# A windowed-attention and ternary-FFN block: output bias added by TensorE, remote bias and gate moved in their queues

## The chip, the core and the metric

The kernel runs on one NeuronCore of one Trainium2 chip. TensorE multiplies matrices and writes to PSUM; VectorE, ScalarE and GpSimd work on SBUF and (but for GpSimd) PSUM; SyncE issues the DMAs. Each engine runs its own instruction list in order, and they wait for each other by semaphores. The metric is the device time of one execution in microseconds.

## The reference

`x` is 16 sequences of 512 tokens of 256 numbers. One transformer block with the norms behind each half:

```
# local attention, 16 heads of 16, window of 128 (the token itself left out), per 128-token block
qkv = x @ qkv_w + qkv_b
local = softmax(where(allowed, q k^T / 4, -1e9)) v            # zero where nothing is allowed
# remote ("latent") attention: 64 pooled chunks of 8 tokens, 4 heads of 16
pooled = mean of x over chunks of 8;  rq = x @ rq_w + rq_b;  rk, rv = split(pooled @ rkv_w + rkv_b)
lat_out = softmax(where(chunk earlier, rq rk^T / 4, -1e9)) rv
remote = lat_out @ rout_w + rout_b                            # split into 16 heads of 16
gate = sigmoid(local @ gl_w + remote @ gr_w)                  # one number per token and head
mixed = gate * local + (1 - gate) * remote
x = layernorm(x + mixed @ out_w + out_b)
# FFN with ternary weights
h = gelu(ternary_linear(x, w_up));  x = layernorm(x + ternary_linear(h, w_down))
```

`ternary_linear` divides its input by its root mean square and multiplies by sign(w) where |w| is over half the mean of |w|, else 0.

## The kernel before

Everything of one sequence fits the chip; the kernel is a software pipeline over the 16 sequences, with the order of each engine's work written out by hand. Steps are named by a phase, a sequence and a number:

- **P** (projections of a sequence, two sequences ahead): `QK`..`QK+3` multiply x by the query and key weights (fp32, four 128x512 products each) into a PSUM bank. The scores need more than bf16 precision, so ScalarE turns each bank into bf16 parts: part 0 at `QK+c`; then TensorE subtracts it from the bank (`SPLIT` steps, a product with `minusb`), ScalarE makes part 1, TensorE subtracts, ScalarE makes part 2. `SPLIT+2t` and `SPLIT+2t+1` belong to tile t. SyncE stores the parts to DRAM and loads them back in stacks (`restack`). Then the latent attention: `LAT_RQ`, `LAT_RKV` (ScalarE: `rqT`, `lat_bd`; VectorE: `rv_bd`), `LAT_SCORES`, `LAT_EXP`, `LAT_NORM`, `LAT_T`, `LAT_O`, and `REMOTE`, `REMOTE+1`, which give `rem` (the remote result) and `remg` (its share of the gate). `VALUES`..`VALUES+3` compute v.
- **A** (22 steps): row maxima of the next sequence's scores, on TensorE and VectorE. `T` is `split_maxima`: they become two bf16 rows, which SyncE puts into the stacks with 16 small DMAs (`move_max`).
- **S, PV** (16 steps): transposed scores, exp on ScalarE, causal masks on GpSimd (`mask`, L656 and L660), weighing of v.
- **F** (second half of a sequence): `GATE` on VectorE (L1146 to L1189) with a tanh on ScalarE (L850), which leaves the mixture transposed in `mixT`; `OUT`, `OUT+1` (TensorE L1558: `mixT` times `wout`; VectorE L1197: adds `xres`, then statistics; GpSimd L670: the powers); `NORM`; `XN_T`, `XN_HI`, `XN_LO`: the normalised input is transposed and split into two f16 parts; GpSimd computes `x1`, the residual's scaling (L676), at `XN_HI`; `UP`..`UP+7` with down products two steps behind (L1544), GpSimd making `h_lo` (L684); `END`.

`SECOND_HALF` (L76) interleaves F of a sequence with P of the sequence two ahead, and all engines follow it. `order_of_prologue` (L133) orders what comes ahead of sequence 0: P of sequences 0 and 1, A of sequence 0, and preparations `W`: `FOLD`, `PREP` (VectorE's `prepare`, L945), `EDGES`, `SUMS`, `TERNARY`. Before sequence 0, ScalarE copies a gate bias at `EDGES`.

The output bias is folded on VectorE at `PREP`: `bout` (in all 128 rows) is out_b plus v's bias times out_w, and GpSimd adds it to the loaded residual `xres`, behind its last mask. Behind that it adds the remote bias of the next sequence:

```
                for b in range(NB):
                    add_bias(s, b)                     # L723, xres += bout, 128x256 each
                if s.next().exists and not s.first:
                    bias_remote(s.next())              # L713, rem += rem_b, two of 128x512
```

Sequence 0 has no such `bias_remote`: that of sequence 1 is in the prologue, at `REMOTE+1`.

## Time and profile before

| | |
|---|---|
| median of 3 runs | 1200.73 us (1200.21 to 1201.3) |
| profiled execution, own time | 1197.75 us |
| its span, first to last instruction | 1196.0 us |
| TensorE, weight loads | 994.4 us (83%), 626.9 us (52%) |
| VectorE, ScalarE, GpSimd | 854.5 us (71%), 744.4 us (62%), 672.6 us (56%) |
| mean granted TensorE clock | 0.960 of full |

In the rows, times are microseconds from the span's start; a row gives start, duration, engine, line, operation, output and input tile, their sizes, and how many alike are merged; in brackets stands how long the engine was idle ahead of it and what ended that. PE is TensorE, DVE VectorE, ACT ScalarE, POOL GpSimd, SPq SyncE's DMA issues. A row that merges several (x4) may span pauses between them.

### The profile page before, as it was taken

What the parts mean: (1) busy time and instruction counts of PE and PEld (TensorE: products, weight loads), DVE (VectorE), ACT (ScalarE), POOL (GpSimd) and SP (SyncE); (2) the same over time, 40 slices, a digit from 0 to 9 for tenths busy, and PEclk for the clock granted to TensorE, in tenths of its full rate; (3) what the DMA queues carried; (4) which work ended last, traced back from release to release, by engine and by line L of the source; (5) the groups of instructions that cost most, each with busy time, mean ns of one, the idle gap of its engine ahead of it and who ended that gap; (6) DMA issues with size and microseconds to landing.
All of it is one profiled execution on the core that took longest, in us unless ns stands there. A gap on an engine that the chain in (4) does not pass through costs nothing. (4 is left out here: it accounts for less than half of the span.)

```text
span 1196.0 us, 36957 instructions
## 1 busy us (share of the span) xinstructions
PE 994.4 (83%) x15353; PEld 626.9 (52%) x15368; DVE 854.5 (71%) x1772; ACT 744.4 (62%) x1189; POOL 672.6 (56%) x852
## 2 busy tenths in 40 slices
PE   6768898988888898888989888888988888894855
PEld 2445564655556464555646455564645555562433
DVE  4377686786868687696868778686877868686454
ACT  3524766767676665767676575757667675763544
POOL 6007375565747465474746646583664648374664
PEclk9888999999999999999999999999999999997877
DMA  6731513315061431506152341515234150601000
GB/s 187 199 98 56 152 46 115 101 46 150 23 177 39 132 83 62 152 15 166 39 153 62 92 123 38 142 39 153 61 98 118 38 143 21 176 22 38 1 18 19
DMA packets 58868, 107.45 MB, mean 90 GB/s; under 512 B 20518, under 2 KB 38726, under 8 KB 55622
## 3 DMA queue, kind: packets, MB, share of 16 engines
q1 hardware_dynamic: 58556, 105.08, 31.1%
q8 instruction: 121, 1.98, 0.7%
q14 instruction: 47, 0.39, 0.1%
q10 hardware_dynamic: 144, 0.00, 0.0%
HBM read 70.87 MB, written 33.55 MB: 87 GB/s over the span
## 5 line engine op out<-in xcount | busy, mean ns | idle before, releaser
L842 ACT ACTIVATE Pt<-scores 128x1024 f32<-128x1024 f32 (+1 forms) x256 | 229.9, 918 | 125.3 <-PE oacc L1531 79.6
L684 POOL TENSOR_TENSOR h_lo<-hbuf,h_hi 128x512 f16<-128x512 f32 x128 | 148.2, 1158 | 202.3 <-DVE h_hi L1231 202.3
L1104 DVE TENSOR_REDUCE nmax<-work 128x3 f32<-128x480 f32 x352 | 214.3, 632 | 28.8 <-PE work L1482 25.8
L656 POOL TENSOR_SCALAR_AFFINE_SELECT Pt<-Pt 128x512 f32<-128x512 f32 x256 | 165.3, 646 | 52.0 <-ACT Pt L842 51.6
L1531 PE MATMUL oacc<-Pt,Vp 128*32 128x256 f32 (+1 forms) x2048 | 152.9, 361 | 15.2 <-POOL Pt L660 9.8
L1361 PE MATMUL scores<-xT,wqk 128*128 128x512 f32 x256 | 125.5, 625 | 37.8 <-ACT parts L762 31.2
L1477 PE MATMUL work<-Ks,Qs 98*32 98x160 bf16 x4096 | 143.6, 235 | 13.2 <-DVE nmax L1104 10.1
L1508 PE MATMUL scores<-Qs,Ks 100*32 100x160 bf16 (+4 forms) x4096 | 118.3, 229 | 32.1 <-ACT Pt L842 17.6
L670 POOL TENSOR_TENSOR rs<-rs,power 128x6 f32<-128x6 f32 x32 | 42.6, 1333 | 176.1 <-DVE rs L1208 176.1
L1231 DVE CAST h_hi<-hbuf 128x512 f16<-128x512 f32 x128 | 68.2, 532 | 101.2 <-ACT hbuf L878 100.7
L1544 PE MATMUL oacc<-wdn_t,h_hi 128*128 128x256 f16 x512 | 118.1, 273 | 9.5 <-POOL h_lo L684 9.5
L660 POOL TENSOR_SCALAR_AFFINE_SELECT Pt<-Pt 128x512 f32<-128x512 f32 x192 | 122.7, 639 | 0.0
L1508 PEld LDWEIGHTS scores<-Qs,Ks 100*32 100x32 bf16 x4096 | 81.2, 97 | 78.6 <-ACT Pt L842 52.1
L1544 PE MATMUL oacc<-wdn_t,h_lo 128*128 128x256 f16 x512 | 117.9, 273 | 0.0
L878 ACT ACTIVATE hbuf<-work 128x512 f32<-128x512 f32 x128 | 76.0, 594 | 60.4 <-PE work L1596 58.9
L1477 PEld LDWEIGHTS work<-Ks,Qs 98*32 98x32 bf16 x4096 | 88.2, 96 | 38.4 <-DVE nmax L1104 27.9
L1596 PE MATMUL work<-xnT,wup_t 128*128 128x512 f16 x384 | 99.4, 381 | 5.7 <-DVE h_sum L1237 5.4
L769 ACT ACTIVATE parts<-scores,bqk 128x512 bf16<-128x512 f32 x128 | 87.7, 685 | 21.3 <-PE scores L1371 15.4
L1482 PE MATMUL work<-mask_band,identb 128*32 128x192 bf16 (+1 forms) x1408 | 99.5, 246 | 0.6 <-issue 0.5
L1237 DVE TENSOR_TENSOR h_sum<-h_sum,work 128x512 f32<-128x512 f32 x112 | 76.3, 682 | 10.8 <-ACT work L885 10.1
L676 POOL TENSOR_SCALAR x<-ytok,mv,rs 128x256 f32<-128x256 f32 x64 | 77.6, 1227 | 1.7
L1343 PE MATMUL scores<-wv,xT 128*128 128x272 f32 x256 | 73.4, 414 | 5.1 <-DVE wrog L972 5.1
(170 smaller groups left out, 1871.6 us busy)
## 6 DMA issues: line engine op xcount, KB each, us to landing
parts_scratch<-parts SPq DMA_DIRECT2D x96, 256.0 KB, 5.2
Qs<-parts_scratch SPq DMA_DIRECT2D x96, 256.0 KB, 4.9
Ks<-parts_scratch SPq DMA_DIRECT2D x96, 256.0 KB, 4.8
xT<-x_t SPq DMA_DIRECT2D x16, 512.0 KB, 3.9
xres<-x SPq DMA_DIRECT2D x16, 512.0 KB, 4.7
y<-nat SPq DMA_DIRECT2D x16, 512.0 KB, 3.0
Qs<-nmax_pair SPq DMA_DIRECT2D x256, 2.0 KB, 1.8
nat<-up_t SPq DMA_DIRECT2D x1, 1024.0 KB, 6.0
```

What stands on the lines that cost most here:

```text
L656: ins = pool.affine_select(out=pt[:, :, 0:P], in_=pt[:, :, 0:P], compare_op=ALU.is_gt, fill=0.0, base=0, pattern=[[0, 4], [1, P]], channel ...
L660: ins = pool.affine_select(out=pt[:, :, P:2 * P], in_=pt[:, :, P:2 * P], compare_op=ALU.is_ge, fill=0.0, base=0, pattern=[[0, 4], [-1, P]] ...
L684: pool.tensor_tensor(h_lo[:, t % NR, :], hbuf[:, t % 2, :], h_hi[:, t % NR, :], ALU.subtract).then_inc(h_lo_ready, 1)
L842: nc.scalar.activation(Pt[:, u % NPT, :, 0:w], scores[:, slot, :, :].rearrange("p k (h q) -> p (k h) q", h=2)[:, :, 0:w], ACT.Exp, scale=S ...
L1104: nc.vector.tensor_reduce(nmax[:, first:first + n], work[:, slot, 0:n * BAND].rearrange("p (h c) -> p h c", h=n), X, ALU.max, negate=True) ...
L1361: mm = nc.tensor.matmul(p_bank(bank), wqk[:, t, c * P:(c + 1) * P], xT[:, t, :], start=(t == 0), stop=False, skip_group_check=True)
L1477: nc.tensor.matmul(work[g * GT:(g + 1) * GT, slot, i * BAND:(i + 1) * BAND], q[0:KA, h, at:at + GT], kk[0:KA, h * S + at:h * S + at + BAND ...
L1482: mm = nc.tensor.matmul(o[:, :, 0:NG + 1:NG, :], identb[:, g * GT:(g + 1) * GT], mask_band[:, :, :].unsqueeze(1).to_broadcast([P, n, 2, GT ...
L1508: mm = nc.tensor.matmul(scores[g * GT:(g + 1) * GT, slot, c // 2, (c % 2) * 2 * P + lo:(c % 2) * 2 * P + hi], kk[0:KB, key + lo:key + lo + ...
L1531: mm = nc.tensor.matmul(oacc[c * PVW:(c + 1) * PVW, hg % 2, j * P:j * P + w], Vp[:, s.par, j, h * VW:h * VW + PVW], Pt[:, v % NPT, c, 0:w] ...
L1544: mm = nc.tensor.matmul(oacc[:, b // 2, (b % 2) * D:(b % 2 + 1) * D], (h_hi, h_lo)[j][:, f % NR, b * P:(b + 1) * P], wdn_t[:, f, :], start ...
L1596: mm = nc.tensor.matmul(work[:, slot, :], wup_t[:, t, f * P:(f + 1) * P], xnT[:, part, t, :], start=(part == 0 and t == 0), stop=(part == ...
```

## The change

1. **Output bias.** GpSimd's `add_bias` is gone. In the prologue VectorE splits `bout` into three bf16 rows (rows 0, 32 and 64 of `bout_rows`, zeros elsewhere), and each OUT step of TensorE ends with two bf16 products of an all-ones `ones_b` with `bout_rows`, into the same PSUM bank. VectorE's addition now waits for the load of `xres` itself.
2. **Remote bias.** `bias_remote` of the next sequence moves on GpSimd from behind the masks to behind `x1` at `XN_HI`.
3. **Gate.** On ScalarE, the tanh (`GATE`) moves from ahead of `QK` to behind `QK`'s part.
4. **Order of the second half.** `QK+3` and `SPLIT+3` move ahead of `OUT`; `SPLIT+6` and `LAT_RQ` ahead of `SPLIT+5` and `OUT+1`.
5. **Prologue.** Loads are in three groups with their own semaphores: for the latent steps, for v's gate column, the rest. `prepare` is cut in two: at `PREP` only v's gate column (four operations); the rest, with the bias rows, in a new step `CONSTANTS` behind sequence 0's `LAT_T+1`, where TensorE's bias products and ScalarE's gate bias move too. The remaining latent steps and values of sequence 1, which stood behind `T`, are spread between the maxima steps.

```diff
@@
 END = UP + FT
 SECOND_HALF = (
     ("F", GATE), ("P", QK), ("P", QK + 1), ("P", SPLIT), ("P", QK + 2), ("P", SPLIT + 1), ("P", SPLIT + 2),
-    ("F", OUT), ("P", QK + 3), ("P", SPLIT + 3), ("P", SPLIT + 4), ("F", OUT + 1), ("P", SPLIT + 5), ("P", SPLIT + 6),
-    ("P", LAT_RQ), ("P", SPLIT + 7), ("P", LAT_RKV), ("P", VALUES), ("P", LAT_SCORES), ("F", NORM),
+    ("P", QK + 3), ("P", SPLIT + 3), ("F", OUT), ("P", SPLIT + 4), ("P", SPLIT + 6), ("P", LAT_RQ), ("P", SPLIT + 5),
+    ("F", OUT + 1), ("P", SPLIT + 7), ("P", LAT_RKV), ("P", VALUES), ("P", LAT_SCORES), ("F", NORM),
     ("F", NORM + 1), ("P", LAT_EXP), ("P", VALUES + 1), ("F", XN_T), ("F", XN_T + 1), ("F", XN_HI),
     ("P", LAT_EXP + 1), ("F", XN_LO), ("P", VALUES + 2), ("F", UP), ("P", LAT_NORM), ("F", UP + 1),
     ("P", VALUES + 3), ("P", LAT_NORM + 1), ("F", UP + 2), ("F", UP + 3), ("P", LAT_T), ("P", LAT_T + 1),
@@
 STAT_AT = 3
 POOL_AT = ("F", UP + 6)
 SPLIT_AT = ("F", UP + 1)
+GATE_AT = ("P", QK)
 NORMALISE_AT = {("F", GATE): (0, 1), ("P", QK + 2): (2, 3)}
 FIRST_HALF = NU + 2
 
@@
 P_RESULTS |= {REMOTE: [R_REM, R_REM + 1], REMOTE + 1: [R_REM + 2]}
 F_RESULTS = {OUT: [("F", 2)], OUT + 1: [("F", 3)], END: [("F", 14)]}
 F_RESULTS |= {UP + f: [("F", 6 + f)] for f in range(FT)}
-FOLD, PREP, EDGES, SUMS, TERNARY = 0, 1, 2, 3, 4
+FOLD, PREP, EDGES, SUMS, TERNARY, CONSTANTS = 0, 1, 2, 3, 4, 5
 AHEAD = 3
 
 
@@
     order += [("P", 0, k) for k in split[6:] + (LAT_RQ, LAT_RKV)] + [("W", 0, PREP), ("W", 0, EDGES)]
     order += [("P", 0, k) for k in (LAT_SCORES, LAT_EXP, LAT_EXP + 1, VALUES, VALUES + 1, LAT_NORM, LAT_NORM + 1,
                                     VALUES + 2, VALUES + 3)]
-    order += [("P", 0, LAT_T), ("P", 0, LAT_T + 1)]
+    order += [("P", 0, LAT_T), ("P", 0, LAT_T + 1), ("W", 0, CONSTANTS)]
     order += [("P", 1, k) for k in split]
     order += [("P", 0, LAT_O), ("P", 1, LAT_RQ), ("P", 1, LAT_RKV), ("W", 0, SUMS)]
-    between = {1: ("P", 0, REMOTE), 3: ("P", 0, REMOTE + 1), 5: ("P", 1, VALUES), 8: ("P", 1, VALUES + 1),
-               17: ("P", 1, LAT_SCORES), 19: ("P", 1, LAT_EXP), 20: ("P", 1, LAT_EXP + 1)}
+    between = {1: [("P", 0, REMOTE)], 3: [("P", 0, REMOTE + 1)], 5: [("P", 1, VALUES)], 7: [("P", 1, LAT_SCORES)],
+               9: [("P", 1, LAT_EXP)], 10: [("P", 1, LAT_EXP + 1)], 12: [("P", 1, VALUES + 1)],
+               13: [("P", 1, LAT_NORM), ("P", 1, LAT_NORM + 1)], 14: [("P", 1, VALUES + 2)],
+               16: [("P", 1, LAT_T), ("P", 1, LAT_T + 1)], 17: [("P", 1, VALUES + 3)], 18: [("P", 1, LAT_O)],
+               20: [("P", 1, REMOTE), ("P", 1, REMOTE + 1)]}
     for v in range(NM):
         order.append(("A", 0, v))
-        if v in between:
-            order.append(between[v])
-    order.append(("T", 0, 0))
-    order += [("P", 1, k) for k in (LAT_NORM, LAT_NORM + 1, VALUES + 2, VALUES + 3)] + [("W", 0, TERNARY)]
-    return order + [("P", 1, k) for k in (LAT_T, LAT_T + 1, LAT_O, REMOTE, REMOTE + 1)]
+        order += between.get(v, [])
+    return order + [("T", 0, 0), ("W", 0, TERNARY)]
 
 
 PROLOGUE = order_of_prologue()
@@
 
         x_in = [sem(f"x_in{k}") for k in range(2)]
         xres_in = sem("xres_in")
-        xres_done = sem("xres_done")
         w_full = [sem(f"w_full{k}") for k in range(2)]
         w_taken = [sem(f"w_taken{k}") for k in range(2)]
         p_full = [sem(f"p_full{k}") for k in range(4)]
@@
             with nc.allow_non_contiguous_dma(reason="bias columns, a few hundred elements"):
                 sp.dma_start(*wqk_load).then_inc(wqk_in, 16)
                 load_x(Seq(0, 0, 0))
+                for dst, src in lat_loads:
+                    sp.dma_start(dst, src).then_inc(w_lat, 16)
+                for dst, src in val_loads:
+                    sp.dma_start(dst, src).then_inc(w_val, 16)
                 for dst, src in loads:
                     sp.dma_start(dst, src).then_inc(w_in, 16)
             load_x(Seq(1, 1, 0))
@@
             link(pool.memset(eps3[:, :, :], EPS))
             link(pool.memset(eps3[:, 1, :], 0.0))
             link(pool.memset(wrog[:, :], 0.0))
+            link(pool.memset(bout_rows[:, :], 0.0))
+            link(pool.memset(ones_b[:, :], 1.0))
             pool.sem_inc(consts, 1)
 
             def rest_of_consts():
@@
                     for b in range(NB):
                         pool.tensor_scalar(x1[:, b, :], ytok[:, b, :], mv[:, b, 0:1], rs[:, 2, b:b + 1],
                                            ALU.subtract, ALU.mult).then_inc(x1_ready, 1)
+                    if s.next().exists and not s.first:
+                        bias_remote(s.next())
                 if UP <= k < END:
 
                     t = k - UP
@@
                                              rem_b[:, t, :].unsqueeze(1).to_broadcast([P, G32, 2 * HD]), ALU.add)
                 ins.then_inc(rem_biased, 1)
 
-            def add_bias(s, b):
-
-                if b == 0:
-                    pool.wait_ge(xres_in, count(s, 1, 0) * 16)
-                if b == 0 and s.first:
-                    pool.wait_ge(bias_ready, 1)
-                pool.tensor_tensor(xres[:, b, :], xres[:, b, :], bout[:, :], ALU.add).then_inc(xres_done, 1)
-
             def finish_before(s):
 
                 pool.wait_ge(var2_ready, count(s, 1, -1))
@@
                     mask(s, u)
                     if u == STAT_AT + NB and not s.first:
                         finish_before(s)
-                for b in range(NB):
-                    add_bias(s, b)
-                if s.next().exists and not s.first:
-                    bias_remote(s.next())
                 for phase, k in SECOND_HALF:
                     if phase == "F":
                         f_step(s, k)
@@
                     if (phase, k) in NORMALISE_AT and not s.first:
                         for b in NORMALISE_AT[phase, k]:
                             normalise_before(s, b)
-                    if phase == "F":
+                    if phase == "F" and k != GATE:
                         f_step(s, k)
-                    elif later.exists:
+                    elif phase == "P" and later.exists:
                         p_step(later, k)
-                    if s.i == B - 2 and (phase, k) == ("F", GATE):
+                    if (phase, k) == GATE_AT:
+                        f_step(s, GATE)
+                    if s.i == B - 2 and (phase, k) == GATE_AT:
                         for u in range(AHEAD):
                             weights(s.next(), u)
 
             def w_step(j):
-                if j == EDGES:
+                if j == CONSTANTS:
                     act.wait_ge(gate_bias, 1)
                     nc.scalar.activation(brg[:, :], oacc[:, 1, 0:1], ACT.Copy).then_inc(gate_bias, 1)
                     act.wait_ge(gate_bias, 2)
@@
             nc.vector.memset(in_pairs(Ks[0])[EXC:PAD + 1], 0.0).then_inc(wide_set, 1)
             nc.vector.memset(in_pairs(Ks[1])[0:ROWS, 0:P // 2], 0.0).then_inc(ones_set, 1)
 
-            def prepare():
+            tmp = ytok[:, 0, :].rearrange("p (h d) -> p h d", h=H)
+            gl3 = glb[:, :].unsqueeze(1).to_broadcast([P, H, HD])
+
+            def prepare_values():
+
+                dve.wait_ge(w_val, W_VAL)
+                for t in range(KT):
+                    link(nc.vector.tensor_tensor(tmp, wv[:, t, :, 0:HD], gl3, ALU.mult))
+                    link(nc.vector.tensor_reduce(wv[:, t, :, HD:VN], tmp, X, ALU.add))
+                dve.sem_inc(prep_done, 1)
+
+            def prepare_constants():
+
                 dve.wait_ge(w_in, W_ALL)
-
-                tmp = ytok[:, 0, :].rearrange("p (h d) -> p h d", h=H)
-                gl3 = glb[:, :].unsqueeze(1).to_broadcast([P, H, HD])
-                gr3 = grb[:, :].unsqueeze(1).to_broadcast([P, H, HD])
-                wro3 = wro[:, :].rearrange("p (h d) -> p h d", h=H)
                 dve.wait_ge(consts, 3)
                 dead3 = dead[:, :, :, :].rearrange("p t m d -> p (t m) d")
                 bv3 = bv_q[:, :, :].rearrange("p t (m d) -> p (t m) d", m=2)
@@
                 link(nc.vector.tensor_reduce(dead3[:, :, HD:VN], few, X, ALU.add))
                 link(nc.vector.tensor_scalar(dead3, dead3, first_row[:, :], None, ALU.mult))
                 nc.vector.tensor_tensor(rem_b[:, :, :], rem_b[:, :, :], bv_q[:, :, :], ALU.subtract)
-                dve.wait_ge(gate_bias, 1)
-                link(nc.vector.tensor_tensor(bout[:, :], bout[:, :], oacc[:, 0, 0:D], ALU.add))
-                dve.sem_inc(bias_ready, 1)
-                for w3, o in [(wv[:, t, :, 0:HD], wv[:, t, :, HD:VN]) for t in range(KT)]:
-                    link(nc.vector.tensor_tensor(tmp, w3, gl3, ALU.mult))
-                    link(nc.vector.tensor_reduce(o, tmp, X, ALU.add))
+                wro3 = wro[:, :].rearrange("p (h d) -> p h d", h=H)
+                gr3 = grb[:, :].unsqueeze(1).to_broadcast([P, H, HD])
                 link(nc.vector.tensor_tensor(tmp, wro3, gr3, ALU.mult))
                 for i in range(2):
                     rows = slice(i * LD, (i + 1) * LD)
@@
                             tmp[rows, :, :].rearrange("p (t h) d -> p t h d", t=KT)[:, t, :, :].rearrange(
                                 "p (c m) d -> p c m d", c=4), X, ALU.add)
                 ins.then_inc(prep_done, 1)
+                dve.wait_ge(gate_bias, 1)
+                link(nc.vector.tensor_tensor(bout[:, :], bout[:, :], oacc[:, 0, 0:D], ALU.add))
+                for k in range(3):
+                    row = slice(k * GT, k * GT + 1)
+                    for j in range(k + 1):
+                        link(nc.vector.tensor_copy(bout_rows[row, :], bout[row, :]))
+                        if j < k:
+                            link(nc.vector.tensor_tensor(bout[row, :], bout[row, :], bout_rows[row, :], ALU.subtract))
+                dve.sem_inc(bias_ready, 1)
 
             def w_step(j):
 
                 if j == FOLD:
 
-                    dve.wait_ge(w_in, W_ALL)
+                    dve.wait_ge(w_lat, W_LAT)
                     dve.wait_ge(consts, 2)
                     nc.vector.tensor_scalar(lat_fold[:, 0, :], diag[:, :], 1.0 / CHUNK, None, ALU.mult)
                     nc.vector.tensor_scalar(lat_fold[:, 1, :], diag[:, :], brk[:, :], None, ALU.mult
                                             ).then_inc(fold_ready, 1)
                 if j == PREP:
-                    prepare()
+                    prepare_values()
+                if j == CONSTANTS:
+                    prepare_constants()
 
                 if j == TERNARY:
                     dve.wait_ge(alpha_all, 1)
@@
                 if OUT <= k < OUT + 2:
 
                     if k == OUT:
-                        dve.wait_ge(xres_done, count(s, NB, NB - 1))
+                        dve.wait_ge(xres_in, count(s, 1, 0) * 16)
                     t = k - OUT
                     slot, n = take(2 + t)
                     blocks = slice(2 * t, 2 * t + 2)
@@
                     pe.wait_ge(mixT_in, count(s, 2, c))
                     slot = work_bank(s, "F", 2 + c)
                     for b in range(2 * c, 2 * c + 2):
-                        mm = product(work[:, slot, (b % 2) * D:(b % 2 + 1) * D],
-                                     lambda t: mixT[:, c, t, (b % 2) * P:(b % 2 + 1) * P], lambda t: wout[:, t, :])
+                        o = work[:, slot, (b % 2) * D:(b % 2 + 1) * D]
+                        for t in range(KT):
+                            nc.tensor.matmul(o, mixT[:, c, t, (b % 2) * P:(b % 2 + 1) * P], wout[:, t, :],
+                                             start=(b % 2 == 0 and t == 0), stop=False, skip_group_check=True)
+                    for b in range(2):
+                        mm = nc.tensor.matmul(work[:, slot, b * D:(b + 1) * D], ones_b[:, :], bout_rows[:, :],
+                                              start=False, stop=True, skip_group_check=True)
                     mm.then_inc(w_full[slot], 1)
                 if XN_T <= k < XN_T + 2:
                     for b in range(2 * (k - XN_T), 2 * (k - XN_T) + 2):
@@
                     step(phase, near[i], k)
 
             for phase, i, k in PROLOGUE:
-                if (phase, k) == ("W", PREP):
+                if (phase, k) == ("W", CONSTANTS):
                     pe.wait_ge(w_in, W_ALL)
                     for t in range(KT):
                         nc.tensor.matmul(oacc[:, 0, 0:D], bv_col[:, t:t + 1].to_broadcast([P, P]), wout[:, t, :],
@@
                         if k == QK:
                             pe.wait_ge(wqk_in, 16)
                         if k == LAT_RQ:
-                            pe.wait_ge(w_in, W_ALL)
+                            pe.wait_ge(w_lat, W_LAT)
                             pe.wait_ge(consts, 2)
                         if k == VALUES:
                             pe.wait_ge(prep_done, 1)
+                        if k == REMOTE + 1:
+                            pe.wait_ge(prep_done, 2)
                         if k == LAT_SCORES:
                             pe.wait_ge(consts, 3)
                     step(phase, START[i], k)
```

## Rows read from the trace of the kernel before

**Rows 1.** Windows: length, busy time of PE, PEld, DVE, ACT, POOL; PE clock; DMA.

```profile
528.20:548.70 20.50, 16.73 (x80) 9.06 (x78) 14.99 (x36) 10.90 (x22) 10.01 (x11) 1.00 0.37 113
...
58.05:78.20 20.15, 15.06 (x342) 9.23 (x342) 17.13 (x29) 5.34 (x9) 2.90 (x3) 1.00 0.62 163
...
78.86:81.82 2.96, 0.00 (x0) 0.00 (x0) 2.86 (x7) 0.25 (x1) 0.00 (x0) 0.65 0.03 2
...
88.51:90.73 2.22, 1.60 (x30) 0.88 (x34) 1.76 (x3) 0.47 (x1) 0.76 (x1) 0.66 0.21 23
...
23.47:25.88 2.41, 2.41 (x10) 1.70 (x9) 0.78 (x3) 1.29 (x4) 2.35 (x2) 0.65 0.95 282
```

**Rows 2.** Timeline of TensorE, sequence 6, behind the attention.

```profile
528.21 3.70 PE L1361 MATMUL scores<-xT,wqk 128*128 128x512 f32 x8
...
534.28 1.88 PE L1361 MATMUL scores<-xT,wqk 128*128 128x512 f32 x4 [2.37 <-ACT parts L762]
...
536.76 1.99 PE L1343 MATMUL work<-wout,mixT 128*128 128x256 f32 x8 [0.17 <-DVE mixT L1188]
```

**Rows 3.** Timeline of ScalarE, same stretch.

```profile
533.16 0.26 ACT L850 ACTIVATE gate<-gate 128x64 f32<-128x64 f32 x1 [5.48 <-DVE gate L1161]
...
546.22 1.28 ACT L785 ACTIVATE lat_bd<-scores,lat_fold 128x64 f32<-128x64 f32 x4
...
548.69 2.08 ACT L859 ACTIVATE mixT<-ytok,nbias,rs 128x256 f32<-128x256 f32 x4 [0.89 <-DVE nbias L1218]
```

**Rows 4.** Timeline of VectorE, same stretch, and the next gate.

```profile
529.10 0.85 DVE L1153 TENSOR_TENSOR o_q<-o_q,dead 128x72 f32<-128x72 f32 x1
...
530.57 1.27 DVE L1156 TENSOR_TENSOR gate<-o_q,gate 128x64 f32<-128x64 f32 x1
...
531.88 1.26 DVE L1161 TENSOR_TENSOR gate<-gate,remg 128x32 f32<-128x32 f32 x2
...
548.42 0.16 DVE L1218 SCALAR_TENSOR_TENSOR nbias<-mv,rs 128x2 f32<-128x2 f32 x1
...
597.46 0.85 DVE L1153 TENSOR_TENSOR o_q<-o_q,dead 128x72 f32<-128x72 f32 x1
```

**Rows 5.** Timeline of GpSimd, same stretch.

```profile
527.76 2.78 POOL L723 TENSOR_TENSOR xres<-xres,bout 128x256 f32<-128x256 f32 x4
...
530.50 2.48 POOL L713 TENSOR_TENSOR rem<-rem,rem_b 128x512 f32<-128x512 f32 x2
...
546.14 4.85 POOL L676 TENSOR_SCALAR x<-ytok,mv,rs 128x256 f32<-128x256 f32 x4
...
556.78 1.16 POOL L684 TENSOR_TENSOR h_lo<-hbuf,h_hi 128x512 f16<-128x512 f32 x1 [5.79 <-DVE h_hi L1231]
```

**Rows 6.** Timelines of VectorE and ScalarE, sequence 0.

```profile
119.25 0.26 DVE L1156 TENSOR_TENSOR gate<-o_q,gate 128x64 f32<-128x64 f32 x1
...
119.55 0.29 DVE L1161 TENSOR_TENSOR gate<-gate,remg 128x32 f32<-128x32 f32 x2
...
135.40 2.08 ACT L859 ACTIVATE mixT<-ytok,nbias,rs 128x256 f32<-128x256 f32 x4 [0.90 <-DVE nbias L1218]
```

**Rows 7.** Timelines of SyncE and TensorE, moved maxima and first scores of sequence 7.

```profile
560.42 11.18 SPq L535 DMA_DIRECT2D Qs<-nmax_pair  x16
...
575.66 0.74 PE L1508 MATMUL scores<-Qs,Ks 100*32 100x160 bf16 x32
```

**Rows 8.** The chain that ended last: a down product of the FFN.

```profile
1113.64 0.87 PE oacc L1544 x8
```

**Rows 9.** Timelines of VectorE, TensorE and SyncE, prologue.

```profile
25.05 0.39 DVE L1055 SCALAR_TENSOR_TENSOR rv_bd<-scores,brv 64x32 f32<-64x32 f32 x2 [7.09 <-ACT lat_bd L785]
...
29.40 0.42 DVE L965 TENSOR_TENSOR ytok<-wv,glb 128x256 f32<-128x256 f32 x1
...
32.71 6.94 PE L1343 MATMUL scores<-wv,xT 128*128 128x272 f32 x16 [5.15 <-DVE wrog L972]
...
79.03 10.02 SPq L535 DMA_DIRECT2D Qs<-nmax_pair  x16
```

25 lines of the change are left out of this document (17 added, 8 removed).

## The prediction

> **What bounds the kernel now.** I read the page first for engine shares, then the granted clock, then the timelines of one middle sequence engine by engine (sequence 6, attention ending near 528 us), then the waits that end in that stretch, and last the prologue.
>
> No engine is full. In the stretch from the last weighing of V to the first normalisation of the FFN input, TensorE is busy 16.73 of 20.50 us at full clock, so 3.77 us are waits [rows 1]. The reader should see what they are. TensorE runs QK and QK+1 from 528.21, then stands idle 2.37 us until 534.28, released by ScalarE's first part [rows 2]; the rest is small. ScalarE could have made that first part long before, but it sits 5.48 us in front of the gate's tanh, which comes first in its order [rows 3]. The tanh waits for VectorE, and there three small additions are long: 0.85 us for 128x72, 1.27 us for 128x64, 1.26 us for a pair of 128x32 [rows 4]. They end where GpSimd's additions end: `xres` plus bias from 527.76 (four in 2.78 us) and `rem` plus bias from 530.50 (two in 2.48 us) [rows 5].
>
> Sequence 0 is the natural experiment: it has no `rem` addition behind its attention. There L1156 takes 0.26 us and L1161's pair 0.29, and the first normalisation starts 16.15 us after L1156 (119.25 to 135.40) [rows 6]; in sequence 6 it is 18.12 us (530.57 to 548.69) [rows 3, 4]. L1156 and L1161 are longer there by 1.98 us together, and 1.97 us arrive at the normalisation. From there on the sequence is one hand-over after another (ScalarE, TensorE, VectorE, GpSimd), and no transfer is waited for: the 16 small transfers of the maxima are issued from 560.42 in 11.18 us, and TensorE first uses them at 575.66 [rows 7]. So what the stretch loses, the period loses.
>
> **The change, part by part.** I count from TensorE's QK (0 = 528.21), for the middle sequences 1 to 13.
>
> *Gate chain on VectorE.* Without GpSimd beside it, L1153 should cost about 0.26 us (L1156's in sequence 0 for about the same size), L1156 0.26, L1161 0.3 [rows 6]. That removes 0.6 + 1.0 + 0.97 = 2.6 us. The gate's sums are ready at 2.35 in place of 4.9.
>
> *ScalarE.* Its first part now precedes the tanh. A QK step of four 128x512 products ends after 1.88 us [rows 2], and the next starts 0.17 us before that end, so the part runs 1.92 to 2.61 and the tanh (0.26) ends at 2.8: 0.2 us of the 2.6 is given back. The transposed mixture of the first half is then ready at 6.1, of the second at 8.7; before, 8.5 and 11.1 (OUT, TensorE's L1343 starts at 536.76, released by it [rows 2]).
>
> *TensorE's order.* QK, QK+1, SPLIT (its part is there), QK+2, SPLIT+1, SPLIT+2 and QK+3 run without a gap to 7.47. SPLIT+3 needs part 1 of the second tile, which ScalarE reaches behind QK+2's part, two normalisations (about 0.54 each) and SPLIT+1: ready at 7.93. So SPLIT+3 at 8.0 and OUT at 8.2. That is hardly earlier than the old 8.55, but QK+3 and SPLIT+3 (1.92 us) now lie before it.
>
> *Bias through TensorE.* Two bf16 products of 128x256 per OUT step. The nearest row is the FFN's f16 product of that shape, eight in 0.87 us, 0.109 each with its weight load [rows 8]: 0.22 per OUT, 0.43 per sequence, all on TensorE's path. VectorE now waits for the raw `xres`, loaded long before.
>
> *The rest of the stretch.* OUT 1.83 and bias to 10.24; SPLIT+4, SPLIT+6, LAT_RQ (0.92), SPLIT+5 to 11.8; OUT+1 with bias to 13.85; SPLIT+7 to 14.06. ScalarE's last part ends at 15.1, `rqT` follows, `lat_bd` (1.28 us, four) ends at 16.9. Before, the same end is 547.50, 19.3 [rows 3]. VectorE's `rv_bd` (0.4 us) waits for it now as before, so the normalisation constants follow it, provided that the second power on GpSimd is done: OUT+1 at 13.85, plus the old distance of 3.4 us (x1 followed the power at 546.14, 17.9 [rows 5], OUT+1 had ended at 14.4), is 17.3, and `rv_bd` ends at 17.4. Normalisation on ScalarE: 18.1 in place of 20.5. **2.4 us per sequence, 13 times, 31.2 us.** Bounds: sequence 0 shows 1.98 for the `rem` addition alone; if the order and the tanh bring only the cost of the bias, 1.55 is left. Above, all idle time of TensorE less the bias: 3.77 - 0.43 = 3.3. I take 2.4, which is inside and comes from the queue.
>
> *`rem` in its new place.* Behind x1's four scalings (4.85 us [rows 5]), from 22.5 to 25.0. GpSimd's next work, the first `h_lo`, came at 556.78 (28.57), now at 26.2. It is hidden by 1.1 us of slack; if that cover goes, the first `h_lo` is late by what exceeds it, and then the first down product. VectorE beside it has only latent work on PSUM, finished by about 21.3.
>
> Here a page reads differently from the trace. In sequence 6 VectorE's normalisation steps run beside x1's scalings on GpSimd: L1218, with two SBUF inputs, takes 0.16 us at 548.42 [rows 4, 5]. So rows price such an encounter at nothing. The Trainium skill, "SBUF — State Buffer", section "Who interferes with whom", says that a VectorE instruction with two SBUF inputs and a GpSimd instruction that reads SBUF exclude each other for the whole instruction, whichever starts second; it fits the three gate additions, but not this row. By it the new normalisation would be held by one or two whole scalings.
>
> *The ends.* Sequence 0 has only L1153's 0.6 and the order to gain: its 18.5 to the normalisation become the 18.1 of the others, -0.4. Sequence 14 has no next projection and waits for transfers before OUT; the bias costs it 0.4 to 0.9: +0.6. Sequence 15: L1153 -0.6, the bias at half clock (an estimate, twice 0.43) 0.85: +0.2.
>
> *Prologue.* Transfers are reordered, but TensorE's first latent product does not wait for them noticeably. Gain: TensorE idles 5.15 us before the first values (32.71), released by VectorE's last constant [rows 9]. Now four operations like L965 (0.42 us, with the gaps 1.9) suffice after `rv_bd` (25.44): 27.3, 5.4 us earlier. Back go the eight bias products, 2.41 us [rows 1], which now precede sequence 1's QK: it starts 3.0 us earlier, and so does the first maxima step. The constants on VectorE (with nine more row operations for the three bf16 rows, about 0.4 each, as L965's 0.42) lie beside TensorE's projections of sequence 1, some 15 us of work, and are hidden; without that cover they would cost up to 8 us. Loss: the rest of sequence 1's latent work moves from behind the maxima to between them. Before, it lay under the maxima's own transfers: 16 issues from 79.03, 10.02 us [rows 9]. VectorE is busy 17.13 of 20.15 us between 58.05 and 78.2 [rows 1]; 2.86 and 1.76 us join [rows 1], 21.75, and the idle 3.0 grows by about 2.0 for the two further value steps, the transposes, LAT_O and REMOTE on TensorE: 26.8, 6.6 more. In addition GpSimd's `rem` addition for sequence 1 (two of 1.24) now falls on VectorE's split of the maxima: the cast and the subtraction, both short, wait for one of them each, about +1.2. Sum 6.6 + 1.2 - 3.0 = **+4.8**. Bounds: with every idle moment filled and no collision -1.4; with nothing of the early start kept about +8.
>
> **The sum.** Against the profiled execution: span 1196.0, own time 1197.75, which is 3.0 below the median 1200.73. The differences: -31.2 - 0.4 + 0.6 + 0.2 + 4.8 = -26.0, so span 1170.0, that execution 1171.7, median 1174.7.
>
> **Rivals.** (A) *ScalarE sets TensorE's pace.* QK+3 and SPLIT+3 stand ahead of OUT, so a ScalarE part that is late delays OUT; ScalarE has 3 parts, a tanh and two normalisations to do in 8 us. For it: SPLIT+3 waits 0.5 us even in my count. Against: ScalarE is busy only 10.90 of 20.50 us [rows 1]. If parts come 1.3 us later, 1.1 is gained per sequence: 1200.7 - 14.3 + 5.2 = 1191.6. (B) *The moved additions meet VectorE elsewhere:* normalisation constants and the first cast are held by one GpSimd scaling (1.21 us) per sequence, 2.4 becomes 1.2: 1200.7 - 15.6 + 5.2 = 1190.3. Against it the 0.16 us row. The rule of the Trainium skill's "SBUF — State Buffer" named above would bring this about. (C) *More comes through:* TensorE closes all gaps, 3.3 per sequence, and the prologue is neutral: 1200.7 - 42.9 + 0.4 = 1158. (D) *Slower.* The long additions are VectorE's own cost in this place and stay; then mixT is ready at 8.5 as before, OUT comes no earlier, and the bias is added: 16 x 0.43 = 6.9, and 4.8, give 1212. It decides if less than 0.9 us per sequence comes through before the bias (6.9 + 4.8 over 13). Against: sequence 0's 0.29. (E) *The transfers of the maxima take over:* they must wait for the restacking transfers ahead of them in SyncE's queue, so that the period stays: 1206. The last issue leaves 575.66 - 571.6 = 4.1 us for landing and to spare, and they start from an event that moves with the stretch [rows 7], so it would need the restack ahead of them to slip by more than 2 us.
>
> **How the numbers follow.** Forecast 0.70; A 0.10; B 0.05; C 0.08; D 0.03; E 0.04. The likeliest: 1174.7. From 1.55 to 3.3 per sequence and -1.4 to +8 in the prologue, the extremes are 1157 and 1189; both ends together are unlikely, so the low end is 1162, and the high end takes A and B in: 1190. A change under 0.2% (2.4 us) can't be told from none here. Faster 0.91 (forecast, A but for its worst 0.02, B, C), same 0.02, slower 0.07 (D, E).
>
> **What would show it.** L1153, L1156 and L1161's pair at 0.26, 0.26 and 0.29 us in all sequences; ScalarE's first part before the tanh, without the 5.5 us idle; no 2.37 us gap on TensorE between QK+1 and QK+2; OUT about 8.2 after QK; the gate's L1153 in neighbouring sequences about 66 us apart in place of 68.4 (529.10 to 597.46 [rows 4]); the first transfer of sequence 0's maxima at about 84 in place of 79.03 [rows 9]. Wrong would make it: a wait of TensorE before SPLIT+3 over 1 us, a first `h_lo` that waits for GpSimd, small VectorE operations near 17 that take over 0.5 us, or a prologue whose maxima end before 78.

## The result, and the profile after

The changed kernel takes 1172.85 us (median of 4, 1169.58 to 1174.39), the one before 1200.47 in the same session (1199.24 to 1201.3): ratio 0.9767, 95% interval 0.9743 to 0.9791. The profiled execution has a span of 1170.0 us, own time 1171.74, mean granted TensorE clock 0.960. Forecast: 1174.7, span 1170.0. The sum came out. Which of its parts earn it is another matter, and the experiments below change the answer.

Sequence 6 of the changed kernel, the stretch of [rows 2 to 5]. TensorE's timeline:

```profile
523.08 3.70 PE L1382 MATMUL scores<-xT,wqk 128*128 128x512 f32 x8
526.62 0.38 PE L1392 MATMUL scores<-parts,minusb 128*128 128x512 bf16 x1
526.83 1.88 PE L1382 MATMUL scores<-xT,wqk 128*128 128x512 f32 x4
...
531.07 0.39 PE L1392 MATMUL scores<-parts,minusb 128*128 128x512 bf16 x1 [0.21 <-ACT parts L774]
531.29 1.89 PE L1581 MATMUL work<-wout,mixT 128*128 128x256 f32 x8
533.02 0.38 PE L1584 MATMUL work<-bout_rows,ones_b 128*128 128x256 bf16 x2
533.24 0.59 PE L1392 MATMUL scores<-parts,minusb 128*128 128x512 bf16 x2
```

The gap of 2.37 us between QK+1 and QK+2 [rows 2] is gone. OUT starts 8.21 behind QK, right behind SPLIT+3, and waits for nothing of its own. The bias products follow it: 0.22 us from start to start of what comes next. ScalarE's and VectorE's timelines of the same stretch:

```profile
525.10 0.69 ACT L767 ACTIVATE parts<-scores,bqk 128x512 bf16<-128x512 f32 x1 [2.68 <-PE scores L1382]
525.68 0.25 ACT L855 ACTIVATE gate<-gate 128x64 f32<-128x64 f32 x1
...
538.54 1.28 ACT L790 ACTIVATE lat_bd<-scores,lat_fold 128x64 f32<-128x64 f32 x4
...
541.01 2.07 ACT L864 ACTIVATE mixT<-ytok,nbias,rs 128x256 f32<-128x256 f32 x4 [0.90 <-DVE nbias L1239]
```

```profile
523.97 0.23 DVE L1174 TENSOR_TENSOR o_q<-o_q,dead 128x72 f32<-128x72 f32 x1
...
524.82 0.26 DVE L1177 TENSOR_TENSOR gate<-o_q,gate 128x64 f32<-128x64 f32 x1
525.12 0.29 DVE L1182 TENSOR_TENSOR gate<-gate,remg 128x32 f32<-128x32 f32 x2
...
528.51 0.71 DVE L1209 STREAM_TRANSPOSE mixT<-x 128x512 f32<-128x512 f32 x1
```

The three gate additions (L1174, L1177 and the pair of L1182, in the kernel before L1153, L1156 and L1161) take 0.23, 0.26 and 0.29 us, against 0.85, 1.27 and 1.26 [rows 4]. That holds in every sequence, by the groups of instructions (busy time in us and mean ns of one behind the bar):

```profile
L1177 DVE TENSOR_TENSOR gate<-o_q,gate 128x64 f32<-128x64 f32 x16 | 4.2, 262 | 0.6
L1174 DVE TENSOR_TENSOR o_q<-o_q,dead 128x72 f32<-128x72 f32 x16 | 3.7, 234 | 0.5
```

Before, sequence 6 was not the only pattern. In sequences 1, 9, 10, 11 and 13 the loss was spread in another way over the same additions, with the same end; sequence 9 of the kernel before:

```profile
735.16 0.23 DVE L1153 TENSOR_TENSOR o_q<-o_q,dead 128x72 f32<-128x72 f32 x1
...
736.02 0.73 DVE L1156 TENSOR_TENSOR gate<-o_q,gate 128x64 f32<-128x64 f32 x1
736.78 2.38 DVE L1161 TENSOR_TENSOR gate<-gate,remg 128x32 f32<-128x32 f32 x2
```

From the start of L1153 to the end of L1161 it is 4.00 us there and 4.03 in sequence 6.

But look at the last row of VectorE's timeline of the changed kernel: the first half of `mixT` is ready at 529.22, and OUT starts at 531.29. The gate chain is now 2.07 us ahead of where it is wanted. The normalisation starts 17.93 us behind QK, before 20.48. GpSimd's remote additions and first `h_lo`:

```profile
545.43 2.49 POOL L730 TENSOR_TENSOR rem<-rem,rem_b 128x512 f32<-128x512 f32 x2
549.19 1.16 POOL L701 TENSOR_TENSOR h_lo<-hbuf,h_hi 128x512 f16<-128x512 f32 x1 [1.27 <-DVE h_hi L1252]
```

GpSimd still waits for VectorE's cast there, so the additions are hidden. The windows of the prologue and, in the last row, of the stretch from QK to the first normalisation, in the columns of [rows 1]:

```profile
20.00:25.00 5.00, 2.89 (x25) 1.85 (x25) 0.00 (x0) 2.99 (x8) 2.83 (x2) 0.65 0.93 305
25.00:28.00 3.00, 2.62 (x11) 1.70 (x12) 2.07 (x6) 0.17 (x1) 2.83 (x4) 0.50 1.01 375
...
38.60:46.00 7.40, 7.40 (x16) 3.18 (x17) 4.58 (x11) 2.18 (x5) 0.00 (x0) 0.77 0.70 205
58.07:84.68 26.61, 19.52 (x368) 12.24 (x368) 21.49 (x37) 8.41 (x15) 3.45 (x4) 0.94 0.46 120
523.08:541.01 17.93, 16.86 (x85) 9.52 (x82) 12.55 (x35) 10.66 (x21) 3.03 (x3) 1.00 0.52 151
```

In the last window TensorE is busy 16.86 of 17.93 us: the stretch now consists almost wholly of its work. The end of the maxima, VectorE, SyncE and TensorE:

```profile
84.96 0.48 DVE L1138 CAST nmax_pair<-nmaxT 128x64 bf16<-128x64 f32 x1
85.47 1.22 DVE L1140 TENSOR_TENSOR nmax_pair<-nmaxT,nmax_pair 128x64 bf16<-128x64 f32 x1
...
86.78 10.02 SPq L544 DMA_DIRECT2D Qs<-nmax_pair  x16
...
98.03 0.72 PE L1529 MATMUL scores<-Qs,Ks 100*32 100x160 bf16 x16 [14.55 <-DMA Qs<-nmax_pair]
```

Measured from gate to gate (start of VectorE's addition of `dead`, L1153 or L1174), the span divides so:

| stretch | before | after | difference | forecast |
|---|---|---|---|---|
| start to gate of sequence 0 | 117.78 | 125.25 | +7.47 | +4.8 |
| sequence 0 to 1 | 66.29 | 66.24 | -0.05 | -0.4 |
| 1 to 14, thirteen periods | 896.53 | 863.05 | -33.48 | -31.2 |
| 14 to 15 | 66.94 | 67.38 | +0.44 | +0.6 |
| 15 to the end | 48.46 | 48.08 | -0.38 | +0.2 |

### The profile page after: what moved, and what is told of

It is laid out like the page before. It is cut to its first block and busy times, and to the rows that moved or that the text cites. A ratio compares the mean times of both kernels' runs of the same rounds, so it can differ in the third digit from the quotient of the medians.

```text
span 1170.0 us, 37047 instructions
## 1 busy us (share of the span) xinstructions
PE 994.1 (85%) x15432; PEld 634.8 (54%) x15432; DVE 823.3 (70%) x1781; ACT 741.7 (63%) x1189; POOL 628.1 (54%) x790
## 5 line engine op out<-in xcount | busy, mean ns | idle before, releaser
L1498 PE MATMUL work<-Ks,Qs 98*32 98x160 bf16 x4096 | 146.3, 236 | 14.5 <-DVE nmax L1125 10.5
L774 ACT ACTIVATE parts<-scores,bqk 128x512 bf16<-128x512 f32 x128 | 86.2, 685 | 49.6 <-PE scores L1392 47.3
L1498 PEld LDWEIGHTS work<-Ks,Qs 98*32 98x32 bf16 x4096 | 90.6, 97 | 40.3 <-DVE nmax L1125 26.1
L1382 PEld LDWEIGHTS scores<-xT,wqk 128*128 128x128 f32 x256 | 48.9, 196 | 57.7 <-issue 54.9
L767 ACT ACTIVATE parts<-scores,bqk 128x512 bf16<-128x512 f32 x64 | 43.7, 683 | 55.5 <-PE scores L1382 55.3
```

Of the source, the lines that this page charges most:

```text
L1382: mm = nc.tensor.matmul(p_bank(bank), wqk[:, t, c * P:(c + 1) * P], xT[:, t, :], start=(t == 0), stop=False, skip_group_check=True)
L1498: nc.tensor.matmul(work[g * GT:(g + 1) * GT, slot, i * BAND:(i + 1) * BAND], q[0:KA, h, at:at + GT], kk[0:KA, h * S + at:h * S + at + BAND ...
```

## The experiments

The theory from here on, P: the steady gain is VectorE's additions freed of GpSimd's, above all of the remote bias; the prologue loses by the latent steps between the maxima. Rivals: the order of the second half, the gate's place, or the bias on TensorE carries it. In the summary, "maxima" is the start of the first maxima step on VectorE and "transfer" that of the first transfer of the maxima; the period goes from the gate of sequence 1 to that of 14, divided by 13; "stretch" is the time from TensorE's QK to ScalarE's first normalisation, the mean of sequences 1 to 13:

| run | median us | ratio, interval | maxima | transfer | period | stretch |
|---|---|---|---|---|---|---|
| before | 1200.5 | 1 | 58.05 | 79.03 | 68.96 | 20.77 |
| after | 1172.85 | 0.9743 to 0.9791 | 58.07 | 86.78 | 66.39 | 18.01 |
| e1_old_between | 1164.59 | 0.9673 to 0.9740 | 57.42 | 79.61 | 66.34 | 18.01 |
| e2_remote_only | 1169.08 | 0.9708 to 0.9782 | 58.32 | 79.30 | 66.71 | 18.47 |
| e3_bias_only | 1184.67 | 0.9843 to 0.9909 | 61.29 | 84.74 | 67.57 | 19.18 |
| e4_old_order | 1176.86 | 0.9778 to 0.9850 | 57.60 | 87.50 | 66.97 | 18.45 |
| g5_gate_first | 1170.85 | 0.9728 to 0.9770 | 57.21 | 84.79 | 66.45 | 18.01 |
| g6_remote_back | 1169.00 | 0.9727 to 0.9757 | 57.78 | 85.63 | 66.17 | 18.02 |
| g7_products_early | 1162.17 | 0.9667 to 0.9701 | 56.19 | 77.18 | 66.61 | 18.01 |
| h8_remote_order | 1158.50 | 0.9615 to 0.9667 | 55.87 | 76.85 | 65.86 | 17.63 |
| h9_parts_stored_first | 1163.09 | 0.9652 to 0.9701 | 55.07 | 76.06 | 66.35 | 18.00 |
| i1_products_doubled | 1167.65 | 0.9713 to 0.9764 | 54.84 | 75.83 | 66.69 | 18.44 |
| i2_bias_back | 1155.81 | 0.9600 to 0.9641 | 57.51 | 78.49 | 65.96 | 17.57 |
| i3_best_store | 1157.66 | 0.9623 to 0.9665 | 57.85 | 78.83 | 65.93 | 17.61 |

The columns are not equally steady. The changed kernel, e1, g5, g7 and h9 differ in the prologue or in the gate's place alone: their stretches agree within 0.01 us, while their periods scatter from 66.34 to 66.61. So the stretch decides between small differences. The transfer has a scatter of its own: e1 and i1 have the same prologue but for one memset, and start it at 79.61 and 75.83. The traces show where that comes from. From the first maxima step to the transfer it takes 20.98 or 20.99 us in all eight kernels with the old places whose granted clock is 1.00 there, and 22.19 in e1, at a mean of 0.92; the other 2.58 us lie before the maxima, where QK and QK+1 take 6.01 us in e1, part of them at the lower of TensorE's two clock levels (1.2 of 2.4 GHz), and 3.70 in i1.

### e1_old_between: sequence 1's latent steps back behind the maxima

```diff
-    between = {1: [("P", 0, REMOTE)], ..., 7: [("P", 1, LAT_SCORES)], 9: [("P", 1, LAT_EXP)], ...}
+    between = {1: [("P", 0, REMOTE)], 3: [("P", 0, REMOTE + 1)], 5: [("P", 1, VALUES)], 8: [("P", 1, VALUES + 1)],
+               17: [("P", 1, LAT_SCORES)], 19: [("P", 1, LAT_EXP)], 20: [("P", 1, LAT_EXP + 1)]}
```

and the rest of them behind `T`, as before.

> The changed kernel, but the remaining latent steps and values of sequence 1 stand behind the split of the maxima again, as before the change (the constants stay in their new step). Theory P (the move itself cost the time): the maxima stretch shrinks from 27.2 to about 20.1 us and GpSimd's remote addition no longer meets the split, 1.3 us; the first transfer of the maxima goes out near 79.2 in place of 86.8, and the time falls by 7.6 us to about 1165. Rival Q (the loss is the constants' new place and TensorE's low clock there): the transfers still start after 84 and the time stays above 1170.

1164.59 us, 8.3 less than the change; the first transfer at 79.61, 7.2 earlier, and the period unmoved. The new places cost what the transfer lost. P held.

### e2_remote_only and e3_bias_only: one part each, on the kernel before

```diff
-                if s.next().exists and not s.first:     # behind the masks
-                    bias_remote(s.next())
+                    if s.next().exists and not s.first: # behind x1
+                        bias_remote(s.next())
```

> The kernel before, with one change: the remote bias moves behind x1 on GpSimd. Theory P (sums of waits as forecast): L1156 and the pair of L1161 fall to 0.26 and 0.3 us, 1.97 us per sequence arrive at the normalisation in 13 sequences, 25.6 us: about 1175. Rival R (the wait is hidden behind TensorE's own queue): under 10 us, over 1190.

e3 takes only the output bias through TensorE (`add_bias` gone, two products in each OUT, the bf16 rows made on VectorE at `SUMS`).

> The kernel before, with one change: the output bias through TensorE as three bf16 rows, no addition to xres on GpSimd (the rows are made in the step SUMS of the prologue, where VectorE is idle). The remote additions then start about 2.8 us earlier on GpSimd. Theory P: they still meet VectorE's first gate addition, which waits for the second of them, but not L1156 and L1161, so 1.3 of the 2.6 us go, less 0.43 us of bias products: 0.9 per sequence, about 1188. Rival R (each VectorE addition still waits for one): no gain, and the bias products cost 6: about 1206.

One moved pair of additions gives 1169.08 us, where 1175 was expected: no less of a gain than the whole change (the intervals of the two ratios overlap). Its gate on VectorE:

```profile
516.55 0.85 DVE L1153 TENSOR_TENSOR o_q<-o_q,dead 128x72 f32<-128x72 f32 x1
517.44 0.55 DVE L1155 RECIPROCAL gate<-o_q 128x64 f32<-128x64 f32 x1
518.03 0.27 DVE L1156 TENSOR_TENSOR gate<-o_q,gate 128x64 f32<-128x64 f32 x1
518.33 0.29 DVE L1161 TENSOR_TENSOR gate<-gate,remg 128x32 f32<-128x32 f32 x2
```

L1153, still beside the `xres` additions, stays at 0.85; the other two are short, 1.97 us less together. (In five of the thirteen sequences L1153 takes 0.23 and L1156 0.73 instead.) The period falls by 2.25 and the stretch by 2.30 where 1.97 was expected. The bias alone gives 1.39 of the period, in place of 0.9, and 1184.67 us in place of 1188. Its first transfer comes 5.7 us later: 3.2 before the maxima, where VectorE makes the bf16 rows at `SUMS` (57.92 to 61.14), and 2.5 in the maxima, at a granted clock of 0.79 (before 1.00). In e3 the remote addition takes the place of the `xres` ones, 2.8 us earlier, and meets L1153's counterpart:

```profile
527.41 1.26 DVE L1155 TENSOR_TENSOR o_q<-o_q,dead 128x72 f32<-128x72 f32 x1
...
529.29 0.26 DVE L1158 TENSOR_TENSOR gate<-o_q,gate 128x64 f32<-128x64 f32 x1
```

```profile
526.08 2.50 POOL L716 TENSOR_TENSOR rem<-rem,rem_b 128x512 f32<-128x512 f32 x2
```

So the two parts don't add: each one clears L1156 and the pair of L1161, e2 by putting the remote additions elsewhere, e3 by letting them run 2.8 us earlier. Together they would be 3.64; the change, with the order on top, has 2.57.

### e4_old_order, g5_gate_first, g6_remote_back: one part undone, on the changed kernel

```diff
 e4: SECOND_HALF as before
 g5:
-GATE_AT = ("P", QK)
+GATE_AT = ("F", GATE)
 g6: bias_remote(s.next()) behind the last mask again, in place of behind x1
```

> The changed kernel with the old order of the second half (OUT ahead of QK+3 and SPLIT+3, OUT+1 ahead of SPLIT+5). Theory P (my count of the two queues): OUT then starts 6.2 us behind QK in place of 8.2, but the last part of ScalarE comes 0.3 later and with it lat_bd: 0.3 x 13 = 4 us, about 1177. Rival R (the order carries the gain, since TensorE's queue sets the stretch): over 1 us per sequence, above 1185.

> The changed kernel with the gate's tanh back in front of QK's first part on ScalarE. Theory P: with the gate's sums ready at 2.25 us behind QK's start, the tanh ends by 2.5 and the part at 3.2, still before TensorE asks for it at 3.4; nothing moves, 1173 within 2. Rival R (the 2.37 us gap of TensorE came from this order): a gap returns and 13 x 1 us or more is lost, above 1185.

> The changed kernel with the remote additions back behind GpSimd's last mask (no addition to xres there). Theory P: one VectorE addition of the gate, the first, waits for the second remote addition, about 1.0 to 1.2 us (1.25 us long where the bias alone had moved); the mixture is ready at 7.3 in place of 6.2, still before TensorE reaches OUT at 8.2. So nothing is lost: 1173 within 2. Rival R (all that delays the gate delays the sequence): 13 x 1.0 to 1.2 = 13 to 15 us, about 1187.

The old order costs 0.58 of the period, 0.44 of the stretch and 4.0 us, about what P had (1177); the intervals of the ratios overlap a little, so the stretch is the better evidence. The gate's place is worth nothing that shows (1170.85, the same stretch). Putting the remote bias back costs nothing either, 1169.00 (both medians are a little under P's 1173 within 2, both intervals overlap the change's, and both prologues are 0.3 us and more shorter), although L1174 meets it in sequences 1 to 14; sequence 6:

```profile
521.64 1.25 DVE L1174 TENSOR_TENSOR o_q<-o_q,dead 128x72 f32<-128x72 f32 x1
```

There QK starts at 520.75 and OUT at 528.97, 8.22 behind it, as in the changed kernel. Of the 1.0 us that the gate loses, 0.8 reach `mixT` (ready 6.93 behind QK in place of 6.14), and they go out of the 2.07 us which it was early. With the new order, then, what GpSimd does beside the gate costs nothing as long as it stays within that slack (0.8 us is what g6 tests). That raises the question whether the bias on TensorE buys anything at all.

### g7_products_early and h9_parts_stored_first: where the early start went

(`store(k)` stands for the three stores of parts of half k.) On e1, the eight bias products of TensorE back between LAT_RKV and LAT_SCORES; then SyncE's list as well:

```diff
 g7:
-                if (phase, k) == ("W", CONSTANTS):     # TensorE's list
+                if (phase, k) == ("W", PREP):
 h9, on g7, SyncE's restack:
+                if s.first:
+                    store(0)
+                    store(1)
+                    wait_alone(sp, parts_out, count(s, 2, 1) * 48)
                 for k in range(2):
-                    store(k)
-                    wait_alone(sp, parts_out, count(s, 2, k) * 48)
+                    if not s.first:
+                        store(k)
+                        wait_alone(sp, parts_out, count(s, 2, k) * 48)
```

> As the run with the old places behind the split (e1), and TensorE's eight bias products stand between LAT_RKV and the latent scores again, where it waits 1.6 us for ScalarE (VectorE's constants stay behind LAT_T). Theory P (the early start was lost to TensorE's idle time and its low clock there: latent scores 2.08 us in place of 1.13, QK and QK+1 of sequence 1 5.36 in place of 3.4): the products fill the wait at no cost, sequence 1's QK starts near 36 in place of 38.6 and runs at the full clock, the first transfer of the maxima goes out 2.5 to 5 us earlier than the 79.6 of that run, near 76: 1161. Rival Q (SyncE's stacks of sequence 0, complete near 50, hold the maxima): at most 1 us earlier.

> The run with the old places between the maxima steps and TensorE's bias products early (median 1162.2, first transfer at 77.2), with one more edit in SyncE's list: for sequence 0 all six stores of parts are issued before the first stack load, where the second three stood behind the first six loads. There ScalarE's first part of sequence 1 waited to 41.28 for the store of sequence 0's second half, issued at 32.82. Theory P (that store held QK of sequence 1): the part starts at about 36, the first transfer of the maxima is at 73 to 75, median 1158 to 1160. Rival Q (stacks of sequence 0 come later, and the maxima's start or the loads of sequence 1's stacks take over): the first transfer stays within 1 us of 77.2, median 1161 to 1163.

In the changed kernel, VALUES began at 28.22 (before 32.71; forecast 27.3), but TensorE's granted clock is 0.50 of full from 25 to 28 us and 0.77 from 38.6 to 46 (windows above); before, with the eight products in the wait, it was 0.97 and 0.99. Changed kernel, TensorE:

```profile
25.39 2.08 PE L1424 MATMUL scores<-lat_bd,rqT 64*128 64x256 f32 x8 [1.61 <-issue]
...
38.62 5.36 PE L1382 MATMUL scores<-xT,wqk 128*128 128x512 f32 x8
```

Eight products for QK and QK+1 take 5.36 us, against 3.60 at full clock in g7, where the clock is 1.00 in all of these windows. That looks as if g7's filled wait had kept the clock up, and P of g7 says so. The other runs contradict it. g5, g6 and i2 leave the wait unfilled as the changed kernel does, and their clock is 1.00 from 20 to 38.6 us; i1 leaves it unfilled too, and has 1.00 from 25 to 28 and from 38.6 to 46. The window from 25 to 28 us in g5 and i1, and g5's TensorE:

```profile
25.00:28.00 3.00, 2.44 (x17) 1.65 (x14) 2.71 (x6) 0.00 (x0) 2.83 (x4) 1.00 1.00 368
```

```profile
25.00:28.00 3.00, 1.69 (x13) 1.09 (x13) 2.07 (x6) 0.55 (x2) 2.83 (x4) 1.00 1.01 371
```

```profile
24.58 1.14 PE L1424 MATMUL scores<-lat_bd,rqT 64*128 64x256 f32 x8 [1.61 <-issue]
...
35.81 3.70 PE L1382 MATMUL scores<-xT,wqk 128*128 128x512 f32 x8
```

h9, with the wait filled as in g7, has 0.66 from 20 to 25 and 0.70 from 33 to 38.6. So where the low stretches fall differs between kernels whose list there is the same, and g7's full clock isn't shown to come from its edit.

Something else caps the early start. In g5, g6 and i2 QK begins at 35.81 to 36.02, 4.3 us and more ahead of the 40.35 before, but ScalarE's first part of sequence 1 at 40.98 to 41.33, only 0.9 to 1.3 ahead of its 42.27. The same wait stands in g7. ScalarE of g5, then ScalarE and TensorE of g7:

```profile
40.98 1.27 ACT L767 ACTIVATE parts<-scores,bqk 128x512 bf16<-128x512 f32 x2 [4.89 <-DMA parts_scratch<-parts]
```

```profile
41.28 1.27 ACT L766 ACTIVATE parts<-scores,bqk 128x512 bf16<-128x512 f32 x2 [5.63 <-DMA parts_scratch<-parts]
```

```profile
34.74 3.60 PE L1381 MATMUL scores<-xT,wqk 128*128 128x512 f32 x8
42.25 1.88 PE L1381 MATMUL scores<-xT,wqk 128*128 128x512 f32 x4 [3.91 <-ACT parts L766]
```

Sequence 1's first part may not overwrite sequence 0's until those are stored, and SyncE issues the last three stores at 32.82, behind six stack loads. This wait ends between 40.98 and 41.94 in six runs (e4, g5, g6, g7, i1, i2). h9 removes it (the part runs at 38.98), and QK+3 of sequence 1 ends at 44.69 in place of 46.28; the first maxima step and the first transfer come 1.1 us earlier, and the median is 1163.09, the same as g7. Rival Q of h9 fits better than P.

What is left behind it the clock can still take: in g5, g6 and i2 it is low from about 43 to 46 us, and their maxima begin at 57.21 to 57.78, hardly ahead of the 58.05 before. i1 and h8, new prologue and old, both have a clock of 1.00 from QK to the transfer: 54.84 against 55.87, so 1.0 us of early start arrives.

Of the 2.4 us by which g7's transfer is earlier than e1's, half (1.2) is e1's lower clock in the maxima, and the medians can't be told apart (the intervals overlap). i1, with the products late, starts the maxima 1.35 us earlier still than g7.

### h8_remote_order, i3_best_store: two small parts of the change alone

h8 is the kernel before with e2's move and the new `SECOND_HALF`, nothing else; i3 adds h9's stores.

> The kernel before with two parts of the change: the remote bias of the next sequence behind x1, and the new order of the second half; the output bias stays on GpSimd behind the masks, the gate's tanh and the prologue stay as before. Two additions of the remote bias were what met the gate's long operations; with them gone only the four additions of the output bias lie there, which end before the second gate operation. Theory P (with the remote bias gone from behind the masks, the output bias on TensorE buys nothing in the steady state, and the order buys the rest): a period of 66.2 to 66.4 us from sequence 1 to 14 against 66.71 with the remote bias alone, first transfer of the maxima at 79.3, median 1164 +/- 3. Rival Q (the output bias on TensorE carries a part of its own, and the order has its worth only with it): a period of 66.7 or more, median 1169 or more.

> The kernel before with the remote bias behind x1 and the new order (median 1158.5, first transfer at 76.8), and with sequence 0's six stores of parts all issued before its first stack load. With the same edit on another version the first transfer came from 77.2 to 76.1 and the median stayed within 1 us. Theory P (the stacks of sequence 0 take over from the store): the first transfer at 75.5 to 77, median 1156 to 1159. Rival Q (it holds more here): first transfer before 75, median under 1156.

1158.50, lower than P's range of 1161 to 1167 and 14 us under the change; the period is 65.86, lower than P's 66.2 to 66.4 and below every version with the bias on TensorE (66.17 to 66.69 with the new order). i3 gives 1157.66, no difference; its transfer comes at 78.83, later than P or Q had it and 2 us later than h8's, all of it before the maxima (57.85 against 55.87), where the clock is low from 52.3 to 55.7 in i3 and not in h8.

### i1_products_doubled, i2_bias_back: the price of the bias on TensorE

Both on e1. i1 puts two more products, of zeros, into each OUT; i2 takes the products and the making of their rows out and adds the bias on GpSimd again.

```diff
 i1:
+                    for b in range(2):
+                        nc.tensor.matmul(work[:, slot, b * D:(b + 1) * D], zeros_b[:, :], bout_rows[:, :],
+                                         start=False, stop=False, skip_group_check=True)
 i2:
-                    for b in range(2):
-                        mm = nc.tensor.matmul(work[...], ones_b[:, :], bout_rows[:, :], ...)
+                for b in range(NB):            # GpSimd, behind the last mask
+                    add_bias(s, b)
```

> The changed kernel with the old places between the maxima steps (median 1164.6, period 66.34), with TensorE's bias products doubled: each OUT step has two more products of an all-zeros tile with the bias rows, so that the sums stay. Measured by itself, a pair of such products takes TensorE 0.38 us. Theory P (TensorE sets the stretch from QK to the normalisation, so the products lie on the path): the period grows by 0.4 to 0.85 us, the median to 1170 to 1178. Rival Q (they lie in idle time of TensorE): a period within 0.2 of 66.34, median 1163 to 1167.

> The changed kernel with the old places between the maxima steps (median 1164.6, period 66.34), and the output bias back on GpSimd behind the last mask, out of TensorE's OUT steps; the remote bias stays behind x1, the order and the gate's place stay new. Theory P (with the remote bias gone from behind the masks, the output bias on TensorE is a net cost: 0.38 us a pair on its path against a gate whose slack covers the additions): a period of 65.7 to 66.0, gates first operation 0.85, median 1157 to 1161. Rival Q (the better time of the run with the remote bias and the order alone comes from its prologue or from the gate's place): a period of 66.2 or more, median 1163 or more.

QK and the first normalisation of sequence 6, i2 first and then i1:

```profile
509.12 3.70 PE L1386 MATMUL scores<-xT,wqk 128*128 128x512 f32 x8
...
526.62 0.60 ACT L874 ACTIVATE mixT<-ytok,nbias,rs 128x256 f32<-128x256 f32 x1 [0.90 <-DVE nbias L1243]
```

```profile
514.63 3.70 PE L1383 MATMUL scores<-xT,wqk 128*128 128x512 f32 x8
...
533.00 2.08 ACT L865 ACTIVATE mixT<-ytok,nbias,rs 128x256 f32<-128x256 f32 x4 [0.90 <-DVE nbias L1240]
```

17.50 us with no products, 17.93 with four per sequence (the changed kernel), 18.37 with eight: 0.43 and 0.44, the full time of the products, each time; the means over the thirteen sequences, 17.57, 18.01 and 18.44, say the same. Nothing of it is hidden in this stretch. The periods (65.96, 66.34, 66.69) go the same way, though the step to i1, 0.35, is not far above their scatter of 0.27 and just under P's 0.4. The median moves by -8.8 and +3.1; i1's 1167.65 lies between the ranges of its P and Q, and its interval overlaps e1's. Of the 8.0 us by which i2's span is below e1's, 4.9 are the thirteen periods; 1.8 lie ahead of the first gate (1.2 of them are e1's lower clock in the maxima) and 1.4 in sequence 0 to 1. In i2 the gate's first addition is 0.85 us again in nine of the thirteen sequences and OUT starts 8.22 behind QK all the same. i2, at 1155.81, has the lowest median of all the versions, not to be told from i3 and h8 (the intervals overlap).

## Why the prediction was right, and where it was not

Step by step:

- *Gate chain freed.* Right: 0.23, 0.26, 0.29 in all sequences, the 2.37 us gap gone, the first part ahead of the tanh, OUT at 8.21 (8.2), `lat_bd` done at 16.74 (16.9), normalisation at 17.93 (18.1). 2.55 us there, 2.76 in the mean of the thirteen stretches, 2.57 in the period, forecast 2.4; the thirteen periods gave 33.5 in place of 31.2. The 0.85 of L1153 was read from sequence 6 and doesn't hold in five of the thirteen, but the chain is as long there.
- *Which part earns it* the text left as one chain, and that hid a net loss in it. Of its 2.6 us on VectorE, the 0.6 of L1153 bought nothing (i2: the same OUT). The 2.0 of the remote addition came through in full (e2: 2.25). The order, which brings OUT hardly earlier in the text's own count, is worth 0.58 (e4) to 0.85 (e2 to h8) of the period, 0.44 to 0.84 of the stretch. The bias products were priced rightly, 0.43 on the path, and measure 0.43 and 0.44. Alone they do buy something (e3: 1.39), but the remote move clears the same additions at no such price, and beside it nothing is bought with them.
- *Gate's place on ScalarE.* Counted as a loss of 0.2 that is absorbed. Right: `mixT` is ready at 6.14 against 5.91 in g5, and the stretch is 18.01 in both.
- *`rem` in its new place.* Hidden, right: GpSimd is free 1.27 us ahead of the first `h_lo` (forecast 1.1). The normalisation constants of VectorE run beside x1's first scaling; one of them takes 0.36 us in place of 0.15, at 540.82, and is off the path (the first constants were already out).
- *The ends.* Within 0.6 us each.
- *Prologue, the failing term: the early start of 3.0 us.* The maxima stretch was 26.61 us (26.8 forecast; before 20.15), the collision with GpSimd's addition 1.28 (0.28 on the cast and 1.0 on the subtraction, forecast 1.2). But the first maxima step began at 58.07, as before at 58.05: the step "it starts 3.0 us earlier, and so does the first maxima step" failed. VALUES was 4.5 us earlier (forecast 5.4) and QK 1.7; then QK and QK+1 took 5.36 us, part of them at the lower clock level, and the rest of the lead was gone when QK+3 began (46.18, before 46.15). At full clock the 3.0 could not have come either: where QK was 4.3 us early or more (g5, g6, i2), ScalarE's first part waited for sequence 0's stores to about 41, which leaves at most 1.3 us of lead, and 1.0 arrives at the maxima where the clock is full (i1 against h8). The prediction has no term for that wait. So the first transfer came 7.75 later and the first gate 7.47, not 4.8. The 26.61 is partly luck as well: at a clock of 1.00 the same steps take 25.48 (g5), so the term of 6.6 for the moved steps is 1.3 too high without a low stretch in it. Why the clock is low where it is stays open.
- *Rivals.* A did not come: SPLIT+3 waits 0.21 us, not 1.3. A gain of 2.57 per period excludes B's 1.2, C's 3.3 and E's none, and the short additions exclude D. No rival named the wait for the stores.

The two misses, +2.7 in the prologue and -2.3 in the periods, cancel, with -0.4 from the rest; that the span came out at 1170.0 exactly is partly luck.

The whole change, taken apart by medians in one order of steps: before 1200.5; remote bias moved 1169.1 (-31.4); new order 1158.5 (-10.6); gate's place, split loads and late constants 1155.8 (-2.7, the intervals overlap); output bias on TensorE 1164.6 (+8.8); latent steps between the maxima 1172.85 (+8.3). In another order the shares would differ: g6 shows that the remote move is worth nothing once the output bias is on TensorE and the order is new. The new order alone, with all of GpSimd's additions behind the masks, wasn't run.

Still open: why medians move somewhat more than thirteen periods do (+8.8 against 4.9; part of it is clock in the prologue), and what decides where the low clock falls, which makes the prologue of equal kernels differ by up to 4 us. Not tried: other places for the constants, and sequence 1's latent steps in the idle time between transfer and first scores alone.

## What to carry to other kernels

When one engine's bulk additions collide with another's short critical ones, move the one that meets the critical ones, and look at once at how much slack the freed chain now has: what exceeds the slack is not a gain, and a part that only adds slack and costs work on the engine that has become the bound is a loss. A forecast that gets the sum of a bundle right says nothing of its parts; price each part against the kernel with all the others in. Before you blame a low clock in one trace on an edit, look whether other runs with the same list have it at the same place. And do not give back a transfer's idle time: work that lay beneath it cost 7.7 us here once it was moved ahead.

## What the runs showed of the hardware

- A VectorE addition of two SBUF inputs that meets a GpSimd addition ends 0.05 to 0.09 us behind the end of one: 0.85 us long beside the 128x256 ones (0.72 each), 1.25 beside the 128x512 ones (1.26 each), 0.23 alone. It is a matter of who comes first: in sequences 1 and 9 of the kernel before, L1153 took 0.23 and the GpSimd addition that began 0.03 us behind it 0.78 in place of 0.72. The reciprocal between, of one input, takes 0.55 us in every run, with `xres` additions beside it or not. The Trainium skill, "SBUF — State Buffer", section "Who interferes with whom", says that a VectorE instruction with two SBUF inputs and a GpSimd instruction that reads SBUF exclude each other. These rows agree with it; the operation of two inputs beside x1's first scaling (L1239 of the changed kernel, at 540.75; the scaling runs from 540.62 to 541.85) does not, with 0.16 us.
- The same TensorE products took 1.13 us (full clock) and 2.08 (granted clock 0.50, after a stretch in which the engine was busy 2.89 of 5.00 us). How busy it was before doesn't tell the two apart: in g5 it was busy 2.29 of the same 5.00 us and the clock stayed at 1.00. Filling the wait before them isn't shown to keep the clock up.
- From the first maxima step to the transfer it took 20.98 or 20.99 us in eight kernels at a granted clock of 1.00, and 22.19 in e1, where the clock was at its lower level for 3.4 us of it (69.5 to 72.9): 1.2 us more.
- Two bf16 products of 128x256 in a stream take 0.22 us, in every place read here at full clock, and all of it shows in the stretch from QK to the normalisation, where TensorE is busy 16.86 of 17.93 us.
